# A hardware loop over six images against the same six bodies written out, in a float32 convolution, attention and feed-forward kernel

## The chip, the cores and the metric

The kernel runs on one core of a Trainium2 chip. The metric is the device time of one execution in microseconds, and the reported figure is the median of several runs. Five engines take part: TensorE (PE in the profile; its weight loads are PEld), VectorE (DVE), ScalarE (ACT), GpSimd (POOL) and SyncE (SP), which here only issues DMAs.

## The reference

The input is a batch of 8 images of 256 channels and 32 x 32 pixels, in float32. Three blocks follow each other:

```python
x = x + proj(attention(group_norm(x)))     # 8 heads of 32 channels, 1024 positions, softmax over keys
t = tokens(x)
t = t + linear_attention(ln(t))            # q, k = elu(ln(t) @ Wqk + b) + 1, rope, kv, lepe convolution
t = t + haar_ffn(ln(t))                    # only the ll band: interpolate, fc1, gelu, fc2, inverse transform
```

The images are independent of each other. The dear part is the first attention: 8 heads x 1024 x 1024 scores per image.

## The kernel before, in words

All matrices stay float32; the scores use a split of q and k into a high and a low part (fp32r), stacked along the contraction. Work is cut into 64 **units** per image: a unit is one head and one block of 128 keys, against all 1024 queries. In unit s PE computes two 128x512 products into one of two score buffers (`scores`, line 570), VectorE takes the negated row maximum (`maximum`, line 937), ScalarE takes the exponential with its sum (`exponentials`, line 805), and once per four units PE multiplies the probabilities with the scaled values (`weigh_values`, line 585). PE works one unit ahead: in the last unit of an image it already computes the first scores of the next one. GpSimd scales the values (line 1213) and issues the load of the next image (`load_image`, line 394, in unit 29).

Everything else is hung into the units by hand. Tables such as `PE_POST`, `ACT_POST`, `DVE_POST` and `POOL_POST` say in which unit each tile of the **previous** image's later blocks is handled; `..._NEAR` holds tiles of this image's second head group, and `..._AHEAD` tiles of the next image: its group norm statistics (`gn_statistics`, line 952, units 34 to 36), its projections (`project_heads`, line 597; `project_values`, line 609). In units 28 and 33 PE computes the `kv` products of the linear attention (line 674), 64 small products each, which the profile records as 128 matmuls with 128 weight loads.

Each engine runs the same sequence: a prologue, the body of image 0 ("first", with no previous image), the body of images 1 to 6 ("steady"), the body of image 7 ("last", with no next image) and an epilogue with the last image's later blocks. The body is one Python function per engine. Image 0 and image 7 are called with a Python number. Images 1 to 6 are one body inside a loop that runs on each engine (`eng.Fori`), with the image index in a register. The whole body is a straight list of instructions; only the image index is variable. It stands in every semaphore wait (`wait_ge(scores_ready, UNITS * i + s + 1)`), in the DRAM addresses of the loads and stores, and nowhere else: on-chip buffers do not depend on it. Semaphores are never reset, they count up over the whole kernel.
The queue of SyncE issues, in each body, the stacking DMAs of q and k (`stack_q`, `stack_k`), the load of the residual, the spread of the band and the stores. The loop is at line 461, in `bodies`, which each of the five engines' blocks calls.

Of the kernel before, what the change touches and what calls it, by code (L numbers as in the profile page):

```python
# [14 lines left out]
B, C, L = 8, 256, 1024  # L15
# [176 lines left out]
def build(nc, x, wqkv_t, wproj_t, wqk, fc1_t, fc2_t, params, consts, out):  # L192
    with ExitStack() as ctx:
# [263 lines left out]
        def bodies(eng, prologue, body, epilogue):  # L457

            prologue()
            body("first", 0, False, True)  # L460
            with eng.Fori(1, B - 1) as i:
                body("steady", i, True, True)
            body("last", B - 1, True, False)
            writing["epilogue"] = True
            epilogue()
            writing["epilogue"] = False
# [3 lines left out]
        def _(sp):  # L470
# [61 lines left out]
            def epilogue():  # L532
# [6 lines left out]
                sp.wait_ge(stored, NC * DMA * B)  # L539

            bodies(sp, prologue, body, epilogue)

        @block.tensor
        def _(pe):
# [240 lines left out]
            def epilogue():  # L786
# [3 lines left out]
                for s in range(UNITS):  # L790
                    post_slot("epilogue", B, s)

            bodies(pe, prologue, body, epilogue)

        @block.scalar
        def _(act):
# [122 lines left out]
            def epilogue():  # L920
                for half in range(2):
                    copy_attention(B - 1, 1, half)
                for s in range(UNITS):
                    post_slot("epilogue", B, s)

            bodies(act, prologue, body, epilogue)

# [489 lines left out]
```

## Time and profile before

| | us |
|---|---|
| median of 3 runs | 1504.45 (1497.10 to 1507.12) |
| the profiled execution's own time | 1496.43 |
| its span, first to last instruction | 1494.8 |
| mean granted TensorE clock | 0.938 |
| from the first exponential of one image to that of the next: image 1 | 170.72 |
| the same, images 2 to 6 | 177.63, 174.39, 177.07, 174.79, 176.91 |

The profile is one execution. Its own time is 1.6 us above its span, and 8 us below the median of the runs. Start times in the rows are microseconds from the start of the span. The exponentials of an image's units mark its place in time: that of unit 0 starts at 184.36 us in image 1, at 355.08, 532.71, 707.10, 884.17 and 1058.96 us in images 2 to 6, and at 1235.87 us in image 7. Where a stretch is named by units, it runs from the start of the first unit's exponential to the start of the one behind the last unit. "issue" as a releaser means that the engine waited for nothing that the profile shows.

### The profile page before, as it was taken

Reading aid. Unit: us, or ns where it says so; the run is one execution under the profiler, and the core shown is the slowest. Engines: PE = TensorE matmul, PEld = TensorE weight load, DVE = VectorE, ACT = ScalarE, POOL = GpSimd, SP = SyncE. Lnnn points to the kernel's source line nnn. Section 1 sums busy time; section 2 is a strip of 40 time slices with the busy share of each in tenths; the row PEclk is TensorE's granted clock in tenths of the full one; section 3 lists DMA queues with packets and bytes.
Section 4 is the critical chain, followed back from the end, with each engine's and each line's share of the span. In section 5 each row is a group of like instructions: output and inputs, shape, how many; then the busy total and the mean of one; then the engine's idle time right before and its main releaser. Section 6 shows DMA issues by size and latency. Waiting matters only on the chain.

```text
span 1494.8 us, 23542 instructions
## 1 busy us (share of the span) xinstructions
PE 1233.8 (83%) x7724; PEld 627.4 (42%) x7724; DVE 995.0 (67%) x1607; ACT 879.0 (59%) x1457; POOL 468.7 (31%) x623
## 2 busy tenths in 40 slices
PE   5787799797978888787987879878897899979856
PEld 4333344344434344443544434444443444434343
DVE  2665587845778477766777567784677758684561
ACT  1656577564765657565675647746575666756412
POOL 2001016510464006530174203640056301641360
PEclk9887899998999999999999999999999999999977
DMA  7242223223242223332142232412234312420111
GB/s 249 48 108 69 66 63 79 76 57 100 57 114 61 51 74 83 87 85 76 37 97 73 73 100 57 111 41 66 81 69 102 85 43 75 94 59 2 43 28 43
DMA packets 51344, 111.31 MB, mean 74 GB/s; under 512 B 15504, under 2 KB 15760, under 8 KB 50992
## 3 DMA queue, kind: packets, MB, share of 16 engines
q1 hardware_dynamic: 48576, 100.85, 27.9%
q0 software_dynamic: 2480, 8.78, 1.9%
q8 instruction: 77, 1.26, 0.4%
q10 hardware_dynamic: 192, 0.26, 0.1%
q14 instruction: 19, 0.16, 0.0%
HBM read 21.75 MB, written 8.39 MB: 20 GB/s over the span
## 4 chain that ended last, share of the span: by engine, by line
PE 49%; DVE 22%; issue 14%; ACT 7%; SPq 4%; DMA 2%; POOL 1%; DVEq 0%; ACTq 0%; POOLq 0%
PE ps_o L585 11%; PE ps_s L570 11%; DVE negmax L937 10%; ACT probs L805 4%; PE work L716 4%; PE work L597 4%; PE work L721 4%; PE work L609 4%; PE work L658 3%; PE work L644 3%; DVE ln_st L1002 3%; DVE tok L1013 2%; SPq L417 2%; DVE t L1087 1%; ACT t L869 1%
## 5 line engine op out<-in xcount | busy, mean ns | idle before, releaser
L937 DVE TENSOR_REDUCE negmax<-ps_s 128x1 f32<-128x1024 f32 x512 | 620.4, 1216 | 328.7 <-PE ps_s L570 327.3
L805 ACT ACTIVATE probs<-ps_s,negmax 128x1024 f32<-128x1024 f32 x512 | 569.8, 1113 | 416.7 <-DVE negmax L937 412.7
L570 PE MATMUL ps_s<-q_st,k_st 128*128 128x512 f32 x1024 | 416.3, 493 | 148.1 <-ACT probs L805 98.8
L570 PEld LDWEIGHTS ps_s<-q_st,k_st 128*128 128x128 f32 x1024 | 172.5, 197 | 396.3 <-ACT probs L805 231.7
L585 PE MATMUL ps_o<-probs,v_scaled 128*32 128x512 f32 x2048 | 271.2, 651 | 6.0 <-POOL v_scaled L1213 6.0
L1213 POOL TENSOR_TENSOR v_scaled<-v_tok,rsums 128x128 f32<-128x128 f32 x128 | 51.6, 403 | 652.4 <-DVE rsums L943 651.3
L597 PE MATMUL work<-xg,w_qkv 128*128 128x512 f32 x256 | 121.3, 597 | 2.0 <-DVE t L1087 2.0
L585 PEld LDWEIGHTS ps_o<-probs,v_scaled 128*32 128x32 f32 x2048 | 56.8, 116 | 148.6 <-issue 135.2
L658 PE MATMUL work<-ln_ch,w_qk 128*128 128x512 f32 x232 | 110.8, 600 | 8.0 <-DVE k_ch L1113 8.0
L1272 POOL TENSOR_TENSOR x<-x,csum 128x1024 f32<-128x1024 f32 x45 | 106.5, 2368 | 3.2
L805 ACT ACTIVATION_READ_ACCUMULATOR probs<-ps_s,negmax 128x1 f32 x512 | 99.6, 194 | 0.0
L609 PE MATMUL work<-w_qkv,xg 128*128 128x128 f32 x512 | 74.3, 308 | 14.1 <-DVE lo L982 8.8
L609 PEld LDWEIGHTS work<-w_qkv,xg 128*128 128x128 f32 x512 | 72.4, 223 | 20.3 <-DVE lo L982 12.3
L839 ACT ACTIVATE hi<-work,par 128x512 fp32r<-128x512 f32 x62 | 42.3, 682 | 53.7 <-PE work L597 50.2
L716 PE MATMUL work<-band,w 128*128 128x512 f32 x118 | 59.9, 637 | 11.8 <-ACT band L877 11.8
L597 PEld LDWEIGHTS work<-xg,w_qkv 128*128 128x128 f32 x256 | 46.7, 189 | 47.5 <-issue 39.0
L1244 POOL TENSOR_TENSOR ln_var<-ln_mv,con 128x2 f32<-128x2 f32 x64 | 13.0, 203 | 168.5 <-DVE ln_mv L1007 168.5
L982 DVE SCALAR_TENSOR_TENSOR lo<-work,par,hi 128x512 fp32r<-128x512 f32 x62 | 46.4, 748 | 29.1 <-ACT hi L839 28.3
L658 PEld LDWEIGHTS work<-ln_ch,w_qk 128*128 128x128 f32 x232 | 42.8, 190 | 45.3 <-issue 28.6
L721 PE MATMUL work<-shared,w 128*128 128x512 f32 x128 | 60.3, 598 | 0.9 <-ACT shared L880 0.9
L644 PE MATMUL work<-att,w_proj 128*128 128x512 f32 x120 | 56.4, 594 | 0.0
L1269 POOL TENSOR_SCALAR csum<-ln_ch,par 128x1024 f32<-128x1024 f32 x45 | 54.9, 1221 | 0.4
(143 smaller groups left out, 1362.1 us busy)
## 6 DMA issues: line engine op xcount, KB each, us to landing
q_st<-hi SPq DMA_DIRECT2D x124, 128.0 KB, 2.4
q_st<-lo SPq DMA_DIRECT2D x124, 128.0 KB, 2.4
k_st<-hi SPq DMA_DIRECT2D x240, 64.0 KB, 2.0
k_st<-lo SPq DMA_DIRECT2D x240, 64.0 KB, 2.0
x<-in_x SPq DMA_DIRECT2D x8, 1024.0 KB, 4.9
out_x<-ln_ch SPq DMA_DIRECT2D x16, 512.0 KB, 3.5
xg<-in_x POOLq DMA_DIRECT2D x7, 1024.0 KB, 6.1
t<-shared SPq DMA_DIRECT2D x64, 64.0 KB, 2.3
```

Source lines behind the costliest of these rows:

```text
L570: mm = pe.matmul(ps_s[s % 2][:, half * HALF:half * HALF + HALF], k_st[:, h, j * P:j * P + P], q_st[g][:, h, half * HALF:half * HALF + HALF ...
L585: mm = pe.matmul(ps_o[D * h:D * h + D, cols], v_scaled[:, j % 2, D * h:D * h + D], probs[:, j % 2, h, cols], start=(j == 0), stop=(j == NB ...
L597: mm = pe.matmul(bank(tile)[:, :], w_qkv[:, c, col:col + P], xg[:, c, half * HALF:half * HALF + HALF], start=(c == 0), stop=(c == NC - 1))
L609: mm = pe.matmul(bank(tile)[:, P * n:P * n + P], xg[:, c, P * nb:P * nb + P], w_qkv[:, c, col:col + P], start=(c == 0), stop=(c == NC - 1))
L644: mm = pe.matmul(ps[:, :], w_proj[:, g, P * c:P * c + P], att[:, g, half * HALF:half * HALF + HALF], start=(g == 0), stop=(g == 1))
L658: mm = pe.matmul(ps[:, :], w_qk[:, c, col:col + P], ln_ch[:, c, 1 + half * HALF:1 + half * HALF + HALF], start=(c == 0), stop=(c == NC - 1))
L716: pe.matmul(ps[:, :], w1[:, P * n:P * n + P], band[:, :], start=True, stop=True)\
L721: mm = pe.matmul(ps[:, :], w2[:, k, :], hid[:, k, :], start=(k == 0), stop=(k == 7))
L805: act.activation(probs[:, j % 2, h, :], ps_s[s % 2][:, :], ACT.Exp, bias=negmax[:, s % 4:s % 4 + 1], accum_out=sums[:, j % 2, h:h + 1]).th ...
L937: dve.tensor_reduce(negmax[:, s % 4:s % 4 + 1], ps_s[s % 2][:, :], AX_X, ALU.max, negate=True)\
L1269: pool.tensor_scalar(lepe_product, ln_ch[:, c, tap:tap + L], param("lepe_w", 3 * c + tap), param("lepe_bias", 3 * c + tap), ALU.mult, ALU. ...
L1272: pool.tensor_tensor(x1[:, c, :], x1[:, c, :], lepe_product, ALU.add).then_inc(lepe_step, 1)
```

## The change

The loop on the engines becomes a loop in Python: the six bodies of images 1 to 6 are written out one behind the other, each with its index as a number. Waits and DRAM addresses become constants, the register instructions and the branch go, and each engine's list of instructions for these images is six times as long. The order of the work, the tiles, the buffers and the semaphores stay as they are.

```diff
@@ -458,7 +458,7 @@
 
             prologue()
             body("first", 0, False, True)
-            with eng.Fori(1, B - 1) as i:
+            for i in range(1, B - 1):
                 body("steady", i, True, True)
             body("last", B - 1, True, False)
             writing["epilogue"] = True
```

## Rows read from the trace of the kernel before

**Rows 1.** The page: busy time by engine; shares of the chain that ended last
```profile
PE 1233.8 (83%) x7724; PEld 627.4 (42%) x7724; DVE 995.0 (67%) x1607; ACT 879.0 (59%) x1457; POOL 468.7 (31%) x623
...
PE 49%; DVE 22%; issue 14%; ACT 7%; SPq 4%; DMA 2%; POOL 1%; DVEq 0%; ACTq 0%; POOLq 0%
```

**Rows 2.** The page, costliest groups: the first
```profile
L937 DVE TENSOR_REDUCE negmax<-ps_s 128x1 f32<-128x1024 f32 x512 | 620.4, 1216 | 328.7 <-PE ps_s L570 327.3
```

**Rows 3.** Timeline of PE: end of image 3 (start, us, what)
```profile
705.07 0.73 PE L570 MATMUL ps_s<-q_st,k_st 128*128 128x512 f32 x2 [0.94 <-DMA k_st<-lo]
710.14 1.22 PE L570 MATMUL ps_s<-q_st,k_st 128*128 128x512 f32 x2 [4.34 <-issue]
```

**Rows 4.** Windows, units 0 and 1, images 1 to 7 (length, busy by engine, PEclk, DMA)
```profile
184.36:188.86 4.50, 4.50 (x40) 3.45 (x42) 3.01 (x5) 2.40 (x4) 0.40 (x1) 1.00 0.38 89
355.08:366.77 11.69, 8.99 (x50) 7.79 (x54) 3.22 (x5) 2.40 (x4) 0.40 (x1) 0.71 0.45 127
532.71:541.31 8.60, 6.24 (x49) 5.00 (x53) 3.22 (x5) 2.41 (x4) 0.40 (x1) 1.00 0.46 134
707.10:717.97 10.87, 7.56 (x50) 6.25 (x54) 3.22 (x5) 2.40 (x4) 0.40 (x1) 0.84 0.46 127
884.17:892.89 8.72, 6.22 (x50) 5.02 (x54) 3.23 (x5) 2.42 (x5) 0.40 (x1) 1.00 0.49 141
1058.96:1069.57 10.61, 7.55 (x50) 6.24 (x54) 3.23 (x5) 2.41 (x4) 0.40 (x1) 0.84 0.40 105
1235.87:1239.80 3.93, 3.93 (x31) 2.72 (x34) 3.02 (x4) 2.40 (x5) 0.40 (x1) 1.00 0.62 207
```

**Rows 5.** Windows, units 2 to 33 of images 1, 4 and 7
```profile
188.86:265.37 76.51, 69.57 (x562) 33.13 (x554) 61.18 (x102) 54.92 (x94) 35.97 (x41) 1.00 0.36 80
...
717.97:794.49 76.52, 69.31 (x562) 32.99 (x554) 61.19 (x102) 54.92 (x95) 36.05 (x41) 1.00 0.35 77
...
1239.80:1316.68 76.88, 69.78 (x562) 32.93 (x554) 61.18 (x102) 54.80 (x94) 36.29 (x41) 1.00 0.36 76
```

**Rows 6.** Windows, units 34 and 35 of images 1, 3, 7 and 0
```profile
265.37:274.88 9.51, 6.06 (x32) 2.78 (x33) 4.57 (x8) 3.36 (x7) 4.57 (x3) 0.82 0.27 75
...
617.87:628.70 10.83, 7.04 (x30) 3.22 (x31) 4.57 (x8) 3.36 (x8) 4.50 (x3) 0.68 0.25 60
...
1316.68:1321.42 4.74, 4.51 (x29) 2.14 (x30) 2.74 (x5) 3.37 (x8) 3.38 (x2) 1.00 0.25 58
111.73:117.43 5.70, 4.81 (x20) 1.29 (x12) 4.15 (x7) 2.88 (x5) 0.00 (x0) 0.65 0.54 106
```

**Rows 7.** Timeline of PE alone, units 33 to 36 of image 1, then of image 7
```profile
263.71 1.59 PE L674 MATMUL work<-tok,shared 128*32 128x32 f32 x128
268.82 0.65 PE L570 MATMUL ps_s<-q_st,k_st 128*128 128x512 f32 x2 [3.52 <-issue]
269.39 3.54 PE L585 MATMUL ps_o<-probs,v_scaled 128*32 128x512 f32 x16
...
1316.81 0.73 PE L570 MATMUL ps_s<-q_st,k_st 128*128 128x512 f32 x2 [0.31 <-ACT probs L805]
```

**Rows 8.** Timeline of VectorE alone, units 34 to 36 of image 1
```profile
266.37 1.29 DVE L952 BATCH_NORM_STATS2 gn_stats<-xg 128x6 f32<-128x512 f32 x2 [1.03 <-DMA xg<-in_x]
269.50 1.23 DVE L937 TENSOR_REDUCE negmax<-ps_s 128x1 f32<-128x1024 f32 x1 [1.84 <-PE ps_s L570]
...
270.84 0.68 DVE L952 BATCH_NORM_STATS2 gn_stats<-xg 128x6 f32<-128x512 f32 x1
273.62 1.23 DVE L937 TENSOR_REDUCE negmax<-ps_s 128x1 f32<-128x1024 f32 x1 [2.10 <-PE ps_s L570]
```

**Rows 9.** DMA queues that carry instructions: first 180 to 350 us, then 875 to 1052 us
```profile
q8 instruction: 8, 0.13, 0.3%
q14 instruction: 6, 0.05, 0.1%
...
q8 instruction: 10, 0.16, 0.4%
```

## The prediction

> **What bounds the kernel now.** I read the page first. No engine is full: PE is busy 83% and VectorE 67% of the span, and the chain that ended last is PE 49%, VectorE 22% and "issue" 14% [rows 1]. The last is time in which an engine waits for nothing the profile shows, so it could be the work of the engines' own sequencers, which is all that this change touches. Inside a unit the chain is PE, VectorE, ScalarE and back to PE: VectorE's maximum takes 1.216 us and idles 327.3 us in all behind PE's scores [rows 2]. Whatever delays one scores product thus delays the image. Next I cut the span by image, as the table of times shows: image 1 takes 170.72 us, images 2 to 6 take 174.4 to 177.6. Six passes of one body differ only where the pass begins: images 2 to 6 come in over the loop's back edge, image 1 falls in from above. That asks for two comparisons, made with windows: the first units of each image, and steady images (register waits) against image 7, whose units up to 33 hold the same work with constant waits.
>
> **Part A, the five back edges.** At the end of image 3, PE issues scores at 705.07 and the next pair at 710.14, with 4.34 us idle, releaser "issue" [rows 3]. No semaphore held it; the loop's branch lies between the two. Units 0 and 1 of images 2 to 6 take 11.69, 8.60, 10.87, 8.72 and 10.61 us, sum 50.49; image 1 takes 4.50 and image 7, with constants, 3.93 [rows 4]. [...] Written out, these units should look like image 7's: 50.49 - 5 x 3.93 = 30.8 us less; against image 1's, 50.49 - 5 x 4.50 = 28.0. I take 29. Is something else late next? The unit's own chain resumes at once in image 7. The DMAs that fill the second half of k are needed only from unit 16 on, some 30 us later, and units 2 to 33 take 76.5 us after a short start (image 1) as after a long one (image 4) [rows 5]. So I let nothing be given back, with 25 us as the low end.
>
 The constants gain nothing there, if anything they lose 0.3 us. Units 36 to 63 have no twin, because image 7 has no next image; I take 0, with 0.4 us either way per image as bounds, 2.4 in all. If the cover were gone, "issue" would stand in front of VectorE and ScalarE, and it does not.
>
> **Part C, a stall that recurs in unit 34.** Units 34 and 35 take 9.51 to 10.83 us in the six steady images (two of them shown), 4.74 in image 7, 5.70 in image 0 [rows 6]. Some of that is honest work: three statistics of the next image's x on VectorE, which image 7 lacks. The rest is on PE: right after the 128 matmuls and 128 weight loads of the second `kv` product, done in 1.59 us, PE stops for 3.52 us with "issue" in the middle of one scores pair; the `weigh_values` behind it then takes 3.54 us, at a granted clock of 0.82 for the stretch. Image 7 has the same burst and goes on after 0.31 us [rows 6, 7]. My reading: PE ran out of instructions. The instruction queue q8 moves 8 packets of 16 KB in image 1 and the like, some 1900 matmuls and loads per image, thus one packet for about 240 [rows 9]. The burst uses up a whole packet in 1.6 us, while the 1 MB load of the next image fills the DMA engines (it lands at 266.37, where VectorE waits 1.03 us for it [rows 8]). It strikes in all six images since the loop's code lies at the same addresses each time, so a packet's edge always falls just behind the burst. Written out, each body's edges fall elsewhere; I count on five of six images being free of it.
> What is one worth? Without the stall the maximum of unit 35 begins when the statistics end, 266.37 + 1.29 = 267.66 in place of 269.50: 1.8 us, the low end. Behind it come 1.23 us of maximum, about 0.3 of `kv` scaling and 0.68 of statistics, so unit 36's maximum could begin at about 269.9 in place of 273.62 [rows 8]: 3.7 us, the high end. I take 3.0, since GpSimd's turning of q is late next. 5 x 3.0 = 15 us; bounds 0 (it stays everywhere) and 6 x 3.7 = 22.
>
> **Part D, the longer code.** The other engines' instructions come over q14: 6 packets in image 1, none in 875 to 1052 us, where the loop body is already on chip; PE refetches, with 10 packets there [rows 9]. Written out, all engines fetch in all images. Image 1 does just this and is the shortest of the six, so I take 0 for it; DMA traffic of 6 packets per image is nothing beside 75 GB/s. The price if it were exposed is a rival below.
>
> **The sum.** 29 + 0 + 15 + 0 = 44 us. From the profiled execution's 1496.4 us that makes 1452. It lies 8 us below the median of the runs shown; taking the 44 from that median gives 1460, which I predict.
>
> **Rivals.**
> *Only the back edges go.* The stall of unit 34 may be no matter of code addresses but of the 1 MB load alone, which still comes in unit 29, or new stalls of the same kind may appear at other bursts. For it: a transfer fills the queues at that very time. Against: PE was held by no transfer of data, and image 7 shows the burst without it. Then 1504.45 - 29 = about 1476. [...]
> *The gain is given back.* PE starts an image 5 us earlier, but the k stacking, on SyncE's queue, lands when it landed: the scores at 705.07 already waited 0.94 us for it [rows 3]. Then each image's edge gives back what it gained, and the time is about 1497 to 1504. Against: that wait lies before the branch, and the stacking is issued behind work that moves with the image.
> *Slower: exposed fetches.* If each of the q14 packets that the loop saves now stops its engine as PE is stopped at the branch, 5 images x 6 packets x 3.5 us = 105 us come on top of the 44 saved: about 1565. It decides from 13 of 30 packets on, where 44 us are eaten. Against it: image 1 and image 7 fetch so and show nothing of it.
> *The program does not change in effect*, for instance if the branch was cheap and the idle time belonged to the image's start: excluded by image 1 and image 7, which have that start and no idle time [rows 4].
>
> **How the numbers follow.** Forecast (both gains, 1450 to 1470): 0.58. Only the back edges (1471 to 1480): 0.26. More than both (below 1450): 0.06. Given back: 0.05. Slower: 0.05. The range reaches from 1446, where B and C lie at their high ends, to 1479, where C is 0 and A is 25: that leaves the two last cases and a tail, under 2 in 10. About 1% (15 us) is what a measurement of this kernel can tell from no change. Faster by over 1%: 0.91; within: 0.05; slower: 0.04.
>
> **What would show it.** Right if units 0 and 1 take about 4 us in each of images 2 to 6 at a clock of 1.00, if units 2 to 33 stay at 76.5 to 76.9, if units 34 and 35 fall to 6 to 7 us in most images and keep about 10 in the one where an edge meets the burst, and if q14 carries some 6 packets in each image and q8 about 8. Part C is wrong if all six still show "issue" of 3 us before the second matmul of that scores pair; D is wrong if "issue" of over 1 us appears before VectorE or ScalarE.

## The result, and the profile after

The written-out kernel takes 1458.84 us (median of 4 runs, 1458.17 to 1461.83), the loop kernel 1503.31 us in the same comparison: ratio 0.9712, interval 0.9675 to 0.975. The forecast was 1460, range 1446 to 1479. The profiled execution of the written-out kernel took 1459.4 us, its span is 1457.6 us, 37.2 less than before. The medians differ by 44.5, 7 more than the spans, because the profiled execution of the loop kernel was a short one of its kind (1496.4 against a median of 1503). The accounting below is between the two spans. Two single executions of later kernels, of 1620 and 4008 us, lie far above the others of the same kernel and are left out of the ratios, though not of the medians.

The page of the kernel after, the lines that answer to [rows 1]:

```profile
PE 1228.9 (84%) x7724; PEld 621.8 (43%) x7724; DVE 993.8 (68%) x1607; ACT 878.9 (60%) x1457; POOL 468.6 (32%) x623
...
PE 49%; DVE 24%; ACT 8%; issue 6%; SPq 5%; DMA 4%; POOL 2%; DVEq 0%; ACTq 0%; POOLq 0%
```

The work is the same; "issue" has gone from 14% of the chain to 6%, and VectorE's share has risen from 22 to 24%. Windows of the kernel after, units 0 and 1 of images 1, 2 and 4, as in [rows 4]:

```profile
186.49:191.35 4.86, 4.86 (x44) 3.81 (x46) 3.11 (x4) 2.40 (x4) 0.40 (x1) 1.00 0.39 91
355.11:359.26 4.15, 4.15 (x37) 3.09 (x40) 3.02 (x4) 2.40 (x4) 0.40 (x1) 1.00 0.67 204
...
690.11:694.09 3.98, 3.98 (x32) 2.77 (x34) 3.01 (x4) 2.40 (x4) 0.40 (x1) 1.00 0.68 204
```

All six take 3.98 to 4.86 us at a granted clock of 1.00, where images 2 to 6 took 8.60 to 11.69 at 0.71 to 1.00 [rows 4]. PE's timeline at the end of image 1 ([rows 3] show the end of image 3):

```profile
352.70 1.17 PE L570 MATMUL ps_s<-q_st,k_st 128*128 128x512 f32 x4 [0.49 <-DMA k_st<-lo]
353.70 3.73 PE L609 MATMUL work<-w_qkv,xg 128*128 128x128 f32 x32
```

The scores pairs on both sides of the image's edge now run as one (x4, 1.17 us), and the 32 value products behind them without a break, where at the end of image 3 there were 4.34 us of "issue" [rows 3]. Windows of the kernel after, units 2 to 33 of images 1 and 4, then units 34 and 35 of all six, as in [rows 5] and [rows 6]:

```profile
191.35:268.17 76.82, 69.45 (x562) 32.81 (x554) 61.18 (x102) 54.88 (x94) 36.30 (x42) 1.00 0.35 78
...
694.09:770.99 76.90, 69.58 (x561) 32.86 (x553) 61.18 (x102) 54.90 (x95) 36.34 (x42) 1.00 0.37 83
```

```profile
268.17:274.12 5.95, 3.91 (x23) 1.55 (x24) 4.42 (x7) 3.37 (x7) 4.20 (x2) 1.00 0.45 114
436.13:442.33 6.20, 3.91 (x23) 1.54 (x24) 4.42 (x7) 3.36 (x7) 4.18 (x2) 1.00 0.45 105
603.87:610.73 6.86, 3.91 (x23) 1.54 (x24) 4.42 (x7) 3.37 (x7) 4.18 (x2) 1.00 0.37 95
770.99:781.19 10.20, 6.27 (x33) 3.08 (x34) 4.63 (x8) 3.36 (x8) 4.14 (x2) 0.83 0.25 63
945.44:951.78 6.34, 3.91 (x23) 1.55 (x24) 4.42 (x7) 3.36 (x8) 4.17 (x2) 1.00 0.43 98
1112.16:1118.10 5.94, 3.91 (x23) 1.55 (x24) 4.42 (x7) 3.37 (x8) 4.19 (x2) 1.00 0.44 103
```

Units 2 to 33 take 0.3 us longer than with registers, as image 7's did before. Units 34 and 35 fall from about 10 to about 6.3 us in five images; image 4 keeps 10.20. PE's timeline there shows the stall of [rows 7], at another instruction:

```profile
769.32 1.41 PE L674 MATMUL work<-tok,shared 128*32 128x32 f32 x127
774.92 0.26 PE L674 MATMUL work<-tok,shared 128*32 128x32 f32 x1 [4.19 <-issue]
...
776.26 2.90 PE L585 MATMUL ps_o<-probs,v_scaled 128*32 128x512 f32 x16
```

It comes one matmul before the end of the burst (127 and then 1), not in the scores pair behind it. The instruction queues during image 4, which answer to [rows 9]:

```profile
q8 instruction: 7, 0.11, 0.3%
q14 instruction: 6, 0.05, 0.1%
```

PE's code comes in 7 packets in place of 10, that of the others in 6 in place of none.

Image by image, measured between the same exponentials and summed over images 1 to 6, the difference is:

| stretch | before | after | difference |
|---|---|---|---|
| units 0 and 1 | 55.0 | 25.1 | -29.9 |
| units 2 to 33 | 459.2 | 461.3 | +2.1 |
| units 34 and 35 | 60.1 | 41.5 | -18.6 |
| units 36 to 45 | 162.4 | 167.5 | +5.2 |
| units 46 to 54 | 172.5 | 177.4 | +4.9 |
| units 55 to 63 | 142.5 | 139.5 | -3.0 |
| sum | 1051.5 | 1012.3 | -39.2 |

Image 1 starts 2.1 us later than before, though nothing ahead of it was changed: in the seven profiles of this text that have the same code ahead of image 1, it starts at 184.4 to 188.7 us. The rest of the span is the same to 0.3 us. Each stretch of the table comes from one execution of each kernel, so differences of a few microseconds in it say little.

### The profile page after: what moved, and what is told of

Same layout as the page of the kernel before. It is cut to its first block, busy times and chain, and to the rows that moved or that the text cites. A ratio compares the mean times of both kernels' runs of the same rounds, so it can differ in the third digit from the quotient of the medians.

```text
span 1457.6 us, 21670 instructions
## 1 busy us (share of the span) xinstructions
PE 1228.9 (84%) x7724; PEld 621.8 (43%) x7724; DVE 993.8 (68%) x1607; ACT 878.9 (60%) x1457; POOL 468.6 (32%) x623
## 3 DMA queue, kind: packets, MB, share of 16 engines
q8 instruction: 62, 1.02, 0.3%
## 4 chain that ended last, share of the span: by engine, by line
PE 49%; DVE 24%; ACT 8%; issue 6%; SPq 5%; DMA 4%; POOL 2%; DVEq 0%; ACTq 0%; POOLq 0%
DVE negmax L937 11%; PE ps_s L570 11%; PE ps_o L585 11%; ACT probs L805 5%; PE work L716 4%; PE work L597 4%; PE work L721 4%; PE work L658 4%; PE work L644 4%; SPq L417 3%; PE work L609 3%; DVE ln_st L1002 3%; DVE tok L1013 3%; DMA xg<-in_x 2%; DVE t L1087 1%
## 5 line engine op out<-in xcount | busy, mean ns | idle before, releaser
L585 PE MATMUL ps_o<-probs,v_scaled 128*32 128x512 f32 x2048 | 264.5, 637 | 5.1 <-POOL v_scaled L1213 5.1
L609 PE MATMUL work<-w_qkv,xg 128*128 128x128 f32 x512 | 67.8, 293 | 8.5 <-DVE lo L982 8.5
L716 PE MATMUL work<-band,w 128*128 128x512 f32 x118 | 63.6, 669 | 12.2 <-ACT band L877 12.2
L609 PEld LDWEIGHTS work<-w_qkv,xg 128*128 128x128 f32 x512 | 66.0, 207 | 14.1 <-DVE lo L982 12.0
L597 PEld LDWEIGHTS work<-xg,w_qkv 128*128 128x128 f32 x256 | 47.1, 190 | 47.6 <-issue 35.0
L869 ACT ACTIVATE t<-work,par_elu 128x512 f32<-128x512 f32 x58 | 39.6, 683 | 26.0 <-PE work L658 26.0
```

The source lines that it names most:

```text
L585: mm = pe.matmul(ps_o[D * h:D * h + D, cols], v_scaled[:, j % 2, D * h:D * h + D], probs[:, j % 2, h, cols], start=(j == 0), stop=(j == NB ...
L597: mm = pe.matmul(bank(tile)[:, :], w_qkv[:, c, col:col + P], xg[:, c, half * HALF:half * HALF + HALF], start=(c == 0), stop=(c == NC - 1))
L609: mm = pe.matmul(bank(tile)[:, P * n:P * n + P], xg[:, c, P * nb:P * nb + P], w_qkv[:, c, col:col + P], start=(c == 0), stop=(c == NC - 1))
L716: pe.matmul(ps[:, :], w1[:, P * n:P * n + P], band[:, :], start=True, stop=True)\
```

## The experiments

They rest on a count of PE's instructions in the trace: matmuls, weight loads and the waits and register instructions of its sequencer. A body has 2093 of them in the loop and 1985 written out. The register instructions are ALU_OP and FUSED_REGOPS in the trace: PE has 702 of them in the loop kernel (594 and 108), VectorE 594, ScalarE 636, GpSimd 432 and SyncE 90, and no engine has one in the written-out kernel. They are fewer than the waits: VectorE runs 98 in image 1, for 174 waits.

All 62 packets of q8 in the written-out kernel have 16384 bytes. For the 9925 instructions of five written-out bodies 39 packets came (`pe_out_only` below), about 254 each. In the six kernels that have PE's bodies written out PE stops 15 times for 0.5 us or more ahead of a matmul or weight load that waits for no semaphore, and all 15 stops stand a multiple of 256 of its instructions apart (2497, 8385, 10433 and 14017 are such places, counted from its first). So I count 256 to a packet. In the loop kernel the six stalls of unit 34 stand 2093 instructions apart, at one place of the body. So the packets' edges fall at the same place of each pass of the loop, and wander by 63 of 256 places from image to image when written out. The loop kernel was run again beside each group of experiments, and the ratios are to those runs: its median was 1498.56 us beside `loop_pad64`, `out_pad64`, `out_pad32` and `single_pass_loops`, 1496.69 beside `pe_out_only`, `rest_out_only`, `loop_hint` and `out_load22`, and 1497.15 beside the other three. The edits are shown against the loop kernel, or against the written-out one where only the load or the instructions of image 0 differ from it.

### Moving the packets' edges, nothing else

Two kernels differ from the loop kernel and from the written-out one only by instructions without work on PE in image 0:

```diff
+        pad_sem = sem("pad_sem")
...
             def body(kind, i, post, ahead):
                 for s in range(UNITS):
+                    if kind == "first" and s < 64:
+                        pe.nop(nofuse=True).then_inc(pad_sem, 1)
                     if s + 1 < UNITS:
```

> The loop kernel, with 64 instructions that do nothing (each only counts up a semaphore of its own) on PE, one ahead of each unit's scores in image 0. They stand before the loop and so shift the whole loop body by a quarter of a 16 KB packet (256 instructions), without a change inside it. Theory (the stall of unit 34 is PE running out of instructions, because a packet's edge lies 2 instructions behind the kv burst in all six images): the 'issue' of 3.3 to 3.7 us in unit 34 is gone in all six images, units 34 and 35 fall from 9.5 to 10.8 us to about 6, unit 36 gives 0.7 us back per image, and the whole is about 14 us faster, 1489. Rival (the 1 MB load of the next image alone makes it): all six stalls stay and the time stays at 1503. Under both, units 0 and 1 of images 2 to 6 stay at 8.5 to 12 us.

Measured: 1484.71 us, ratio to the loop kernel 0.9895 (0.9837 to 0.9954), 13.9 us less by the medians. Windows of this kernel, units 34 and 35 of images 1, 2 and 6:

```profile
265.99:272.02 6.03, 3.91 (x23) 1.55 (x24) 4.36 (x7) 3.36 (x7) 4.62 (x3) 1.00 0.45 120
436.60:443.86 7.26, 3.91 (x23) 1.54 (x24) 4.36 (x7) 3.36 (x7) 4.56 (x3) 1.00 0.37 95
...
1135.17:1141.96 6.79, 3.91 (x22) 1.58 (x23) 4.37 (x7) 3.36 (x7) 4.55 (x3) 0.91 0.40 98
```

The stalls are gone in all six images (6.03 to 7.26 us, where there were 9.51 to 10.83), from a change that lies wholly in image 0. Units 0 and 1 of images 2 to 6 stay slow, at 7.29 to 12.06 (the low end is 1.2 below what was expected). The load of the next image runs as before, so it cannot make the stall alone.

> The written-out kernel with the same 64 instructions on PE in image 0. In the written-out kernel each body is 1985 instructions long on PE, so the packet's edge wanders by 63 of 256 positions from image to image, and meets the end of the second kv burst in image 4 alone. Theory: shifted by 64, it meets it in images 1 and 5 (1 and 3 instructions behind the burst's end) and no longer in image 4: units 34 and 35 take about 10 us in images 1 and 5 and about 6 in the other four, one stall more than now, total about 1462. Rival (something of image 4 itself, or the load): image 4 keeps its 10.2 us and images 1 and 5 their 6, total 1459.

Measured: 1460.08 us. Windows, units 34 and 35 of images 1, 4 and 5:

```profile
260.29:270.00 9.71, 6.18 (x32) 2.83 (x33) 4.62 (x8) 3.36 (x7) 4.15 (x2) 0.82 0.27 69
...
768.91:774.91 6.00, 3.92 (x23) 1.55 (x24) 4.42 (x7) 3.37 (x8) 4.18 (x2) 1.00 0.44 109
936.57:946.32 9.75, 6.37 (x34) 2.92 (x34) 4.63 (x8) 3.37 (x7) 4.14 (x2) 0.82 0.26 63
```

The stall moved to the two images that the count of instructions named and left image 4; the other three take 5.79 to 6.32 us.

The third has `s < 32` in that diff.

> The written-out kernel with 32 such instructions on PE, in the first 32 units of image 0. Theory: the packet's edge is then never within 25 instructions of the burst's end in any of the six images, no image has the stall, units 34 and 35 take 6 to 7 us in all, total about 3 to 4 us less than the written-out kernel, 1455. Rival (the load alone): image 4 keeps 10.2 us, total 1459.

Measured: 1453.24 us (5 runs, 1450.94 to 1462.51), 0.9686 (0.9633 to 0.9739), which is not told apart from the written-out kernel. The profile is of the slowest of the five. Units 34 and 35 take 5.67 to 7.41 us in all six images. No image stops for 3 us inside or just behind the burst, as forecast; image 5 stops for 1.51 us inside the `weigh_values` behind it, where the packet's edge lies 30 instructions behind the burst.

### The jump back, apart from the register waits

```diff
-            with eng.Fori(1, B - 1) as i:
-                body("steady", i, True, True)
+            for n in range(1, B - 1):
+                with eng.Fori(n, n + (2 if n < B - 2 else 1), 2 if n < B - 2 else 1) as i:
+                    body("steady", i, True, True)
```

> The six bodies written out, but each of images 1 to 5 in a loop of its own that runs once, so that every wait of these images is still against a value worked out in a register and every body still ends in a branch, which is never taken back. Only the jump back is gone. Theory (register waits cost nothing, the jump back costs it all): units 0 and 1 take 4 to 5 us, units 2 to 33 76.5 us in images 1 to 5, and the total is within 3 us of the written-out kernel's 1459; the stall of unit 34 shows in image 1 alone, where the code lies as in the loop. Rival (the register instructions cost the 29 us): 1485 or more, with units 0 and 1 still at 8 us or more.

Measured: 1459.28 us, 0.9726 (0.9654 to 0.9798), the written-out kernel's time. Windows: units 0 and 1 of image 2, then units 2 to 33 of image 1:

```profile
356.99:360.91 3.92, 3.92 (x32) 2.77 (x34) 3.01 (x5) 2.39 (x4) 0.40 (x1) 1.00 0.64 211
...
190.79:267.30 76.51, 69.49 (x562) 33.11 (x554) 61.17 (x102) 54.94 (x95) 35.98 (x41) 1.00 0.35 80
```

With register waits in images 1 to 5 the first units are as short as with constants (3.91 to 4.24 us in images 2 to 6). The register waits cost nothing that these runs can tell; the jump back costs it all. The branch instructions of the loop kernel at line 461 show it too, VectorE's and then PE's (count, then shortest, median and longest in ns):

```profile
L461 DVEq COMPARE_BRANCH  x6: 50/56/72, 350.8 to 1231.6; - x6
L461 PEldq COMPARE_BRANCH  x6: 83/4160/4802, 352.0 to 1232.6; - x6
```

PE's five jumps back take 3.40 to 4.80 us, its last branch, which falls through to image 7, 0.083; in `single_pass_loops` each of the six takes 0.10 or less. The jumps of the other engines take 0.07 at most. By the trace's own times of the instruction queue, a packet begins 0.7 to 2.5 us after each of the five branches, and in four of them PE goes on 2.3 to 2.8 us after that packet began (in the first jump two packets follow each other and it takes 3.8). PE's six stalls of unit 34 end in the same way, 2.6 to 2.7 us after a packet began. So in both places the engine goes on when a packet of code has come. One detail was missed: units 34 and 35 are slow in image 1 (9.84 us), as expected, and in image 2 as well (10.09), where the packet's edge lies 44 instructions before the end of the burst.

### Whose jump it is

`pe_out_only` writes out the six bodies for PE alone, `rest_out_only` for the other four engines alone:

```diff
-            with eng.Fori(1, B - 1) as i:
-                body("steady", i, True, True)
+            if eng is nc.tensor:
+                for i in range(1, B - 1):
+                    body("steady", i, True, True)
+            else:
+                with eng.Fori(1, B - 1) as i:
+                    body("steady", i, True, True)
```

> Only PE's six bodies are written out; VectorE, ScalarE, GpSimd and SyncE keep the loop with its register waits and its jump back. Theory (the jump back costs because PE's instructions have to be fetched anew; the others' loop bodies stay on chip): units 0 and 1 take about 4 to 5 us in all images, q14 carries no packets in images 2 to 6, total within 3 us of the written-out kernel's 1459. Rival (the jump of the other engines costs its part too): somewhere between, 1470 to 1490.

> The reverse: PE keeps the loop, the other four engines are written out. Theory: units 0 and 1 of images 2 to 6 stay at 8.5 to 12 us and the stalls of unit 34 stay, total within 5 us of the kernel before, about 1500. Rival (their register waits or jumps cost): 1475 to 1490.

Measured: 1454.45 us, 0.9693 (0.9637 to 0.9748), with PE alone written out; 1504.22 us, 1.0041 (1.0003 to 1.0079), with all others written out, against 1496.69 for the loop kernel beside them. So the whole gain is PE's. The instruction queue of `pe_out_only` in images 2 to 6, and units 0 and 1 of images 2 and 4 in `rest_out_only`:

```profile
q8 instruction: 39, 0.64, 0.3%
```

```profile
361.12:371.97 10.85, 7.67 (x50) 6.44 (x54) 3.24 (x4) 2.41 (x4) 0.40 (x1) 0.70 0.44 123
...
713.31:725.19 11.88, 9.07 (x50) 7.79 (x54) 3.24 (x4) 2.41 (x5) 0.40 (x1) 0.71 0.45 124
```

No q14 line appears in the first: the code of the small engines is not fetched again, and their jumps cost nothing that shows. In the second all of the old cost is there, clock of 0.70 and 0.71 included. It also tells whose constants make units 2 to 33 longer by 0.3 us: they take 76.8 to 76.9 us here, where PE still has its register waits, so at least part of the 0.3 us comes from the constants of the other engines. The medians put `pe_out_only` 4 us below the written-out kernel, but the two ratios to the loop kernel don't tell them apart. In its profile no image has 10 us in units 34 and 35 (at most 8.36), though PE's code and its edges are those of the written-out kernel. The DMA queue in 771.5 to 771.6 us and PE's timeline in image 4 show why:

```profile
q8 instruction: 1, 0.02, 74.5%
```

```profile
775.49 0.73 PE L574 MATMUL ps_s<-q_st,k_st 128*128 128x512 f32 x2 [0.36 <-ACT probs L809]
```

Here the packet began at 771.5 us, 0.4 us ahead of the first data of the load; in the written-out kernel the load's data come 0.4 us earlier against the burst, and the packet follows only behind them (below). PE runs through the burst and waits just 0.36 us, for ScalarE. That these 0.4 us decide it is my reading of the two traces.

> The loop kernel with two bodies in each pass (images 1 and 2, 3 and 4, 5 and 6), so that PE jumps back twice in place of five times; all waits stay register waits. Theory: images 3 and 5 alone begin with units 0 and 1 of 8 to 12 us, images 2, 4 and 6 with about 4.5; and as the second body lies at other addresses than the first, the stall of unit 34 stays in images 1, 3 and 5 (2 instructions behind the burst) and is gone in 2, 4 and 6. Three jumps at 5.6 us and three stalls at about 3 us less: 26 us under the kernel before, about 1471. Rival (the cost belongs to the image's start or to the register waits): no change in the images whose body follows without a jump, 1497.

```diff
-            with eng.Fori(1, B - 1) as i:
+            with eng.Fori(1, B - 2, 2) as i:
                 body("steady", i, True, True)
+                body("steady", i + 1, True, True)
```

Measured: 1485.51 us, 0.9922 (0.9894 to 0.9949): 12 us less, not 26. Windows: units 0 and 1 of images 2, 3 and 4, then units 34 and 35 of image 2; behind them PE's timeline in unit 33 of image 2:

```profile
356.07:359.99 3.92, 3.92 (x32) 2.77 (x34) 3.01 (x5) 2.40 (x5) 0.40 (x1) 1.00 0.59 199
526.75:535.48 8.73, 6.22 (x50) 5.01 (x54) 3.22 (x5) 2.41 (x4) 0.40 (x1) 1.00 0.46 135
701.29:705.79 4.50, 4.50 (x40) 3.45 (x42) 3.01 (x5) 2.40 (x4) 0.40 (x1) 1.00 0.65 196
...
436.57:446.67 10.10, 6.42 (x48) 2.90 (x47) 4.57 (x8) 3.36 (x8) 4.51 (x3) 0.83 0.29 77
```

```profile
434.90 1.18 PE L675 MATMUL work<-tok,shared 128*32 128x32 f32 x112
440.25 0.33 PE L675 MATMUL work<-tok,shared 128*32 128x32 f32 x16 [4.17 <-issue]
```

The jump part holds: images 2, 4 and 6 begin in 3.92 to 4.50 us, and images 3 and 5 in 8.73 and 12.21. The stall part fell: images 2, 4 and 6 keep theirs (9.81 to 10.23), because in them the edge lies 31 instructions before the end of the burst, where I had thought it harmless. In image 2 PE stops after 112 of the 128 matmuls.

### A hint ahead of the jump

The edit puts one more instruction per engine at the top of the body: each of the five engines has it six times in the trace, as BRANCH_PREFETCH_HINT, PE's at 185.6 to 1066.4 us, 36 to 50 ns long. That code for the jump could be fetched ahead of time by it was my assumption. One import line of this edit is not shown.

```diff
-            with eng.Fori(1, B - 1) as i:
+            with nc.Fori(1, B - 1, engines=OrderedEngineSet([eng.engine]), hint_back_edge=True) as i:
```

> [...] Theory (the idle time at the jump is the fetch of PE's code): units 0 and 1 of images 2 to 6 fall from 8.6 to 11.7 us to 4 to 6 us, the idle 'issue' before PE's second scores pair is under 1 us, the stalls of unit 34 stay (the code moves by one instruction only), total 20 to 28 us under the kernel before, about 1478. Rival (the jump itself or the restart of PE costs it): 1500.

Measured: 1506.35 us, 1.0062 (1.0031 to 1.0094), against 1496.69 for the loop kernel beside it. PE's timeline at the end of image 3:

```profile
707.12 0.73 PE L571 MATMUL ps_s<-q_st,k_st 128*128 128x512 f32 x2
710.85 0.72 PE L571 MATMUL ps_s<-q_st,k_st 128*128 128x512 f32 x2 [2.99 <-issue]
711.41 1.27 PE L610 MATMUL work<-w_qkv,xg 128*128 128x128 f32 x10
714.38 2.72 PE L610 MATMUL work<-w_qkv,xg 128*128 128x128 f32 x22 [1.69 <-issue]
```

The theory's forecast failed here: PE still stops at the jump (2.99 us of "issue") and again 32 instructions behind it (1.69). Units 0 and 1 of images 2 to 6 sum to 47.1 us, 3.4 less than without the hint [rows 4]. The hint stands at the top of the body, 2093 instructions or some 8 packets ahead of the jump. Queue q8 carries 74 packets in this kernel and 77 in the loop kernel, so no packet shows that the hint alone would have brought; whether it is taken at all stays open. The experiment speaks neither for nor against the fetch, for which the packets at the jump and the second stall speak. That the median is some 10 us higher fits units 46 to 54, which take 8 us more in this profile at a granted clock of 0.91 in four images (see below); it is no sign of a cost of the hint itself.

### The load's part in the stall

```diff
-    "load": (29,), "squares": (37,), "affine": (37,),
+    "load": (22,), "squares": (37,), "affine": (37,),
```

> The written-out kernel with the 1 MB load of the next image issued by GpSimd in unit 22 instead of 29 (the image's x was last read in unit 20). Theory: the load no longer shares the DMA engines with PE's instruction packet at the second kv burst, and VectorE's statistics in unit 34 no longer wait for it. Image 4's units 34 and 35 fall from 10.2 to about 7 us (an uncontended fetch takes about 1 us less than the burst allows), those of the others from about 6.2 to 5 us; GpSimd's turning of q in unit 36 gives half of it back; total 4 to 8 us less, about 1453. Rival A (the edge alone makes the stall, the load has no part): image 4 keeps 10 us. Rival B: the load now delays something in units 22 to 28, and the time is 1459 or more.

Measured: 1445.74 us, 0.9632 (0.9562 to 0.9702), 13 us under the written-out kernel, more than expected. Windows, units 34 and 35 of images 3 and 4, and PE's timeline in unit 33 of image 4:

```profile
602.84:607.56 4.72, 4.40 (x28) 2.03 (x29) 4.32 (x7) 3.36 (x7) 3.37 (x2) 1.00 0.28 66
767.14:773.09 5.95, 4.65 (x30) 2.24 (x31) 4.44 (x8) 3.36 (x7) 3.37 (x2) 1.00 0.19 45
```

```profile
765.48 1.46 PE L674 MATMUL work<-tok,shared 128*32 128x32 f32 x127
768.34 0.22 PE L674 MATMUL work<-tok,shared 128*32 128x32 f32 x1 [1.40 <-issue]
```

Image 4's edge lies where it did, but PE stops for 1.40 us in place of 4.19. The DMA queues say why. In the written-out kernel, image 4, the first line is the stretch 766 to 772 us and the second 772 to 773:

```profile
q0 software_dynamic: 272, 1.05, 56.2%
...
q8 instruction: 1, 0.02, 7.6%
```

The burst begins at 769.32. While the load moves, no instruction packet does: its data move from 767.2 to 771.5 us, and PE's packet begins at 772.3. With the load in unit 22 the packet moves within 1 us of the burst's start at 765.48. No run shows the fetch that takes 1 us less than the burst allows, which the expectation counted on: the edge at the burst makes a stop of 1.40 us by itself, and the load adds 2.8. Rival A falls. The load also explains the wide range of bad places. In the trace's times of ten kernels with the load in unit 29 there are 60 such loads, and PE's packets begin ahead of the load's first data or up to 0.4 us behind it, or else not before 4.0 us behind it, about when the load ends. With the edge 62 instructions before the burst's end (`loop_pad64`) the packet begins 0.1 to 0.35 us ahead of the load, with the edge 31 or 44 before it (in code with register instructions) only behind the load. In `out_load22` VectorE's statistics no longer wait for the load, by my reading the reason why the other images gain 1.5 us each in units 34 and 35.

> The loop kernel with the 64 instructions in image 0 and the load in unit 22, so everything that was found but the jump. Theory (the parts add up): units 34 and 35 at 4.7 us in all six images, total 8 to 10 us under loop_pad64's 1485, about 1476, and the five jumps alone are left between it and the written-out kernel with load in unit 22 (1446), some 28 to 30 us. Rival (the gain of the early load is used up where the jumps are): no better than 1483.

Measured: 1461.92 us, 0.9755 (0.9709 to 0.9801), 23 us under `loop_pad64`, where I had expected 8 to 10. The two profiled spans differ by 18.6 us: 13.2 in units 34 and 35 (4.67 us in all six), 3.5 in units 36 to 45 and the rest scattered, so some 4 us of the difference of the medians have no place in the profiles. A loop kernel is thus about 3 us from the written-out one with the load in unit 29, with a sixth of its code for the six images.

> The written-out kernel with 32 instructions in image 0 (no packet's edge near the burst) and the load in unit 22. Theory: image 4's units 34 and 35 fall from 5.95 us to 4.73 as in the other images, total 1 to 2 us under the 1446 of the load in unit 22 alone, which the measurement can hardly tell; about 1444. Rival (no image has a stall left that costs, once the load is out of the way): 1446.

Measured: 1442.25 us (6 runs, 1440.03 to 1444.92), 0.963 (0.9595 to 0.9665) of the loop kernel. It is the fastest of all; its difference to `out_load22` is not told apart. Units 34 and 35 take 4.73 to 4.86 us in all images.

## Why the prediction was right, and where not

**Part A, the jumps, held.** 29 us forecast, 29.9 measured in units 0 and 1. `single_pass_loops` and `two_bodies_per_pass` show that it is the jump and not the waits, `pe_out_only` and `rest_out_only` that it is PE's. That the idle time is a fetch of code is shown by the packet inside each jump and by the second stall 32 instructions on, of 0.85, 2.04 and 1.80 us, which three of the five jumps have and which `loop_pad64`, with its edges elsewhere, does not show; the packets of an image also fall from 10 to 7. What PE does in the 2.3 to 2.8 us between the packet's start and its next matmul was not split further.

**Part B, the register instructions, held.** Nothing forecast, +2.1 us measured for units 2 to 33. The bound of 2.4 was meant for units 36 to 63; for units 2 to 33 the prediction had itself read 0.3 us per image from image 7, and left these 2 us out of its sum. The cover is there on three engines: in the loop kernel's trace all 594 register instructions of VectorE (40 ns at the median, 24.5 us in all) run while one of its own instructions computes, 618 of 636 of ScalarE's and 661 of 702 of PE's. Of GpSimd's only 182 of 432 do, so there the prediction's sentence on the cover says too much.

**Part C, the stall, was right in kind, in place and in number.** Five of six images are free of it, one keeps it. Gross it is worth 18.6 us; units 36 to 45 give 5.2 back. In the five images unit 36 takes 3.12 to 3.18 us in place of 2.45, 3.4 us in all; the rest is lost in image 4, whose units 36 to 45 take 28.9 us in place of 27.1 behind its stall. What is late in unit 36 there is not GpSimd's turning of q, as I had named it, but VectorE. Its timeline in the kernel after, image 1:

```profile
274.66 0.23 DVE L1071 TENSOR_SCALAR den<-work 128x64 f32<-128x64 f32 x1 [0.55 <-PE work L691]
274.92 0.55 DVE L1073 RECIPROCAL zden<-den 128x64 f32<-128x64 f32 x1
275.39 0.63 DVE L952 BATCH_NORM_STATS2 gn_stats<-xg 128x6 f32<-128x512 f32 x1
275.94 1.20 DVE L937 TENSOR_REDUCE negmax<-ps_s 128x1 f32<-128x1024 f32 x1
```

The denominators, their reciprocal and a statistic stand ahead of the maximum of unit 37, without a pause behind the first. Net 13.4, forecast 15. The prediction named all three parts of the cause, the edge, the burst and the load, but not what each of them makes: the load adds 2.8 of 4.2 us. The bad places reach from 44 before to 2 behind the burst's end in code with register instructions, not over a few. (Written out, an edge 34 before it, image 4 of `out_pad32`, cost little: 6.80 us.) Its count of five free images out of six was a guess about code whose addresses it didn't have, and came true; with 64 instructions more there are four.

Most edges between packets cost nothing that shows: in images 1 to 6 of the written-out kernel 47 packets begin, and PE stops for 1 us or more inside its work without a semaphore at two places, the one of image 4 (4.19 us) and one of 1.02 us in the first burst of image 6. Beside the second burst they do cost: `loop_pad64` and `out_pad64` moved 3 us stalls by shifting edges alone. The time of the rival *Only the back edges go*, about 1476, did not come.

**Part D, the longer code, held.** No engine shows more idle time under "issue" than before (VectorE 0.2 us after 1.4, ScalarE none after 1.3, GpSimd 0.2 after 2.4), and q14 carries 45 packets in place of 19, 4 to 6 in each image, at no visible cost.

**What the sum left out.** Units 46 to 54 take 4.9 us more. Their time goes with the granted clock: windows of the loop kernel before, images 1 and 3, and of `out_pad32_load22`, images 2 and 3:

```profile
301.94:331.30 29.36, 27.68 (x135) 14.12 (x134) 13.07 (x15) 21.78 (x35) 2.91 (x5) 0.97 0.32 72
...
655.76:683.52 27.76, 26.08 (x128) 12.52 (x126) 13.07 (x15) 21.77 (x34) 2.93 (x5) 1.00 0.35 76
```

```profile
462.31:490.06 27.75, 26.00 (x126) 12.36 (x125) 13.07 (x15) 21.78 (x35) 2.81 (x5) 1.00 0.34 76
626.43:657.40 30.97, 29.23 (x131) 14.21 (x130) 13.07 (x15) 21.78 (x35) 2.81 (x5) 0.91 0.31 68
```

The same work takes 27.75 us at a clock of 1.00 and 30.97 at 0.91. Which images get the lower clock differs from kernel to kernel: of the six none is below 0.97 before, two are at 0.91 after, four in `out_pad32_load22`. What decides it was not tried, and since each kernel was profiled once, it may differ between executions too.

**How near 1460 came, and by what.** Between the profiled spans the jumps gave 29.9 us and the stalls 13.4, 43.3 of the 44 forecast. Then 2.1 us went in units 2 to 33, 4.9 in units 46 to 54 and 2.1 ahead of image 1, and 3.0 came in units 55 to 63, which nobody forecast: 37.2 us. The medians differ by 44.5 because the loop kernel's was 1503.31 in this comparison; beside the experiments it was 1496.69 to 1498.56. So the two large terms were right, and that the total agreed to about 1 us was luck. The low end of the range, 1446, does not follow from its terms either: with B and C at their high ends and A at 29 the median of 1504.45 gives 1451.

**The rivals.** The gain given back at the k stacking did not happen, though that wait is still there (0.49 us at 352.70); exposed fetches of the small engines did not happen.

## What to carry to other kernels

Count how many instructions lie between two points of one engine before judging an idle time that no semaphore explains. Here PE, whose 2093 instructions are fetched anew in each pass of the loop (10 packets in image 5), lost 3.40 to 4.80 us in the branch at each of five jumps back, and some 6 us per jump in units 0 and 1. At its dense burst, where a packet's edge met it, it lost 1.40 us, and 4.19 us while the 1 MB load moved. Move the load away from the burst first; it is one number in a table and was worth 11 to 23 us here. In this kernel only PE, the engine with the long body, had to be written out (1454.45 us, against 1504.22 with only the others written out), and the waits on registers cost nothing that the runs can tell (1459.28 us in `single_pass_loops`, against 1458.84).

## What the runs showed that was not expected

A transfer of 1 MB issued by GpSimd kept a single 16 KB instruction packet of PE back until it was done, some 3 us after the burst began (772.3 against 769.32 us). Instructions without any work, placed in image 0, changed the loop kernel by 14 us. In 60 loads no packet of PE's code began between 0.4 and 4.0 us behind the load's first data. And the hint instruction at the top of a body of 2093 instructions made nothing faster (1506.35 us against 1496.69).
